# Four chained vision layers on one core: each tile's gathers are sent once those of the tile before have landed

## The reference

```python
x = x + moe(gn(x))           # layer 0: 2x2 patches, 8 experts, top 2
x = x + relu(bn(deform(gn(x))))   # layer 1
x = x + ssm_glu(gn(x))       # layer 2: 16-tap state-space convolution, GLU
x = x + convnext(gn(x))      # layer 3: 7x7 depthwise convolution, MLP

def deform(x):
    dy, dx, mask = conv3x3(x, w_om) + b_om         # 9 offsets and 9 masks a pixel
    py, px = base_y + dy, base_x + dx
    # bilinear: four corners of each of the 9 places, at data-dependent indices
    sampled = sum(gather(x, corner) * weight(corner) for corner in four) * sigmoid(mask)
    return einsum('bckhw,ock->bohw', sampled, w) + b
```

## Time and profile before

| | |
|---|---|
| timed runs, median of 3 (lowest to highest) | 1748.08 us (1746.49 to 1748.33) |
| span of the profiled execution | 2176.8 us |
| the profiled execution's own time | no other than its span is given |
| first and last start of a gather, profiled | 78.2 us, 1983.5 us |
| mean granted TensorE clock, profiled | 0.801 of full speed |
| POOL busy, profiled | 1190.0 us, of it gathers 1135.1 us |
| PE, DVE, ACT busy, profiled | 1392.0, 953.2, 526.5 us |

### The profile page before, as it was taken

The page is one execution under the profiler, slowest core; times in us unless marked ns, Lnnn a source line. Parts: engine busy times, 40 slices in busy tenths (PEclk is TensorE's granted clock), DMA queues, the critical chain, the costliest instruction groups (busy, mean ns, idle before and its releaser), DMA issues.

```text
span 2176.8 us, 13143 instructions
## 1 busy us (share of the span) xinstructions
PE 1392.0 (64%) x3780; PEld 595.6 (27%) x3780; DVE 953.2 (44%) x1562; ACT 526.5 (24%) x860; POOL 1190.0 (55%) x1393
## 2 busy tenths in 40 slices
PE   4647554496246877863366878855368874386976
PEld 3433212242112333322122333322123321132322
DVE  2424233354341333884532323875323328532564
ACT  1111111121112233211222333211213322132544
POOL 8655446357665555676565454676645566673000
PEclk9868766698567998986577889977678987687987
DMA  5212212132241111222141111222221112110100
GB/s 192 60 48 68 52 40 62 49 90 59 74 101 41 43 44 43 71 66 58 53 113 46 31 40 39 74 65 58 57 76 35 41 44 57 41 58 26 32 5 18
DMA packets 111591, 123.70 MB, mean 57 GB/s; under 512 B 50720, under 2 KB 88224, under 8 KB 111136
## 3 DMA queue, kind: packets, MB, share of 16 engines
q0 software_dynamic: 36864, 75.57, 12.5%
q1 hardware_dynamic: 73600, 43.82, 8.1%
q10 hardware_dynamic: 1056, 3.47, 0.4%
HBM read 99.79 MB, written 9.01 MB: 50 GB/s over the span
## 4 chain that ended last, share of the span: by engine, by line
PE 36%; another core or an unknown queue 27%; DVE 16%; issue 12%; ACT 7%; DMA 1%; SPq 1%; ACTq 0%; DVEq 0%
PE bank L1795 7%; PE bank L1808 7%; PE bank L1721 4%; DVE rb L1599 3%; PE bank L1717 3%; PE bank L1731 3%; DVE gt L1508 3%; PE bank L1752 2%; PE bank L1831 2%; PE bank L1783 2%; PE bank L1817 1%; DVE he L1406 1%; PE bank L1847 1%; PE bank L1772 1%
## 5 line engine op out<-in xcount | busy, mean ns | idle before, releaser
L1055 POOL DMA_INDIRECT gt<-corner_table,idx x1152 | 1135.1, 985 | 783.8 <-DVE sm L1516 392.4
L1795 PE MATMUL bank<-u,wk 128*128 128x512 f32 x512 | 256.7, 648 | 25.6 <-issue 9.6
L1808 PE MATMUL bank<-yg,wts 128*128 128x512 f32 x512 | 241.6, 615 | 46.9 <-ACT yg L1189 30.2
L1406 DVE SCALAR_TENSOR_TENSOR he<-he,bank 128x512 f32<-128x512 f32 (+1 forms) x144 | 90.2, 627 | 275.4 <-remote 88.9
L1721 PE MATMUL bank<-xg,w_sb 128*128 128x512 f32 (+1 forms) x288 | 149.3, 602 | 85.0 <-DVE xg L1397 61.9
L1772 PE MATMUL bank<-cst,sm 128*128 128x128 f32 x384 | 80.0, 322 | 187.0 <-ACT st L1173 79.7
L1540 DVE SCALAR_TENSOR_TENSOR tg<-tg,ae 128x512 f32<-128x512 f32 x64 | 44.5, 696 | 344.3 <-ACT ae L1201 270.9
L1731 PE MATMUL bank<-he,w_sb 128*128 128x512 f32 (+1 forms) x288 | 143.0, 580 | 54.6 <-DVE he L1406 30.9
L1508 DVE TENSOR_TENSOR gt<-gt,bank 128x1152 f32<-128x1152 f32 x128 | 172.5, 1347 | 0.9
L1599 DVE SCALAR_TENSOR_TENSOR rb<-xp,par,rb 128x1024 f32<-128x1024 f32 x124 | 155.1, 1291 | 0.0
L1125 ACT ACTIVATE he<-bank 128x512 f32<-128x512 f32 (+1 forms) x144 | 78.8, 549 | 294.3 <-PE bank L1717 166.7
(11 more groups left out here) (222 smaller groups left out, 1390.2 us busy)
## 6 DMA issues: line engine op xcount, KB each, us to landing
gt<-corner_table,idx POOLq DMA_INDIRECT x1152
tb<-gate_of_token SPq DMA_DIRECT2D x32, 256.0 KB
sqb<-gate_of_token SPq DMA_DIRECT2D x24, 256.0 KB
u<-sqb SPq DMA_DIRECT2D x48, 128.0 KB
corner_table<-tb SPq DMA_DIRECT2D x36, 128.0 KB, 2.7
w_sb<-w ACTq DMA_DIRECT2D x2, 1024.0 KB, 6.7
sqb<-gate_of_token SPq DMA_DIRECT2D x16, 128.0 KB
u<-xg SPq DMA_DIRECT2D x16, 128.0 KB
```

What stands on the lines that cost most here:

```text
L1055: pool.indirect_dma_start(gt[:, t % GRING, k].rearrange("p a c -> p (a c)"), None, corners, bass.IndirectOffsetOnAxis(ap=idx[s % 2][:, j, ...
L1406: stt(out=he[:, u % 2, 0:w], in0=he[:, u % 2, 0:w], scalar=1.0, in1=psum[b][:, 0:w], op0=ALU.add, op1=ALU.mult).then_inc(free[b], 1)
L1795: op = mm(psum[b][:, :], wk[:, t, d], u4[:, g, at:at + HALF], start=t == 0, stop=t == JJ - 1 and n > 0)
L1808: op = mm(psum[B2.bank(*name)][:, :], w_glu[:, k, col + d * P:col + (d + 1) * P], yg[:, c % 2, k], start=k == 0, stop=k == NB2 - 1)
```

## The change

Before the nine gathers of a tile, POOL also waits until all nine of the preceding tile have landed. `u` is the running number of the preceding tile, and its semaphore has by then been raised nine times by 16 in each of its `u // GRING + 1` turns. The first tile of step 0 has none before it.

```diff
                 if s or t >= GRING:
 
                     pool.wait_ge(S["smp_ready"], FROM + s * NT * GI + t - GRING + 1)
+                if s or t:
+                    u = s * NT * GI + t - 1
+                    pool.wait_ge(gathered[u % GRING], (u // GRING + 1) * 16 * KK)
                 for k in range(KK):
                     pool.indirect_dma_start(
```

## The result

The changed kernel takes **2044.3 us** (2042.62 to 2048.8, 4 runs) beside 1748.2 us for the kernel before in the same session: 1.1702 times, 95% interval 1.1683 to 1.1722. It is 296 us slower. The forecast was slower, at 1896 us with a range up to 1930. Half of the loss was foreseen.

The account below looks back on a forecast made before the run. POOL, sending gathers nearly without a pause, was taken as the bound; 1748.1 us + 146 for 120 paying waits + 10 for late landings - 8 absorbed = 1896 us, range 1765 to 1930 us (its own range 1860 to 1930).

Parts of the forecast that it names:

- What bounds the kernel: In timed runs POOL sends gathers nearly without a pause, one each 1.25 us; its summed time is 1738 us.
- Rival (1): The wait is hidden because the timed POOL is not the bound: 1748 to 1751 us; chance 0.13.
- The wait itself costs nothing: The added wait instruction on POOL, one among waits already there before a tile's first gather, was put at nothing.
- What one wait costs: At a tile boundary on POOL, 1.52 us instead of the 0.30 us gap: 1.22 us a tile.
- Late landings: Gathers queued behind SP's `u4` loads may land up to 10 us late; 10 us taken, bounds 0 and 60.
- How many pay: Of 127 added waits, 7 run under POOL's waits for table or indices; 120 pay, 146 us.
- Absorbed by POOL's idle time: The idle time POOL still has in timed runs, 10 us, absorbs 8 us of the cost.
- Rival (3): The landing is told late, as for SP's table store: 1.73 us a tile, 208 us, 1956 us; chance 0.04.
- What is late next: Nothing new: each tile reaches DVE 1.2 us later, and the 192 us after the last tile move as a whole.
- the ring: POOL's ring of four buffers doesn't help, since it lets POOL run ahead only if POOL is the faster one.
- Rival (2): POOL bounds some stretches, PE or DVE the others: 1821 us with half the boundaries, 1765 to 1855; chance 0.17.
- What the profile would show: Gaps between tiles at least about 1.4 us, inside tiles 0.30; profiled span up by perhaps 0 to 60 us.

Follow-up runs that it names:

- second profile: The kernel before, unchanged, run and profiled once more: 1751.0 us, 1.0011 times, with a profiled span of 1749.2 us.
- the run with eight gathers: Ninth gather left out from the fifth tile on, against the kernel before: 1718.8 us, 0.9832 times; with the change's wait as well, 1888.7 us, 1.0817 times.

## Why the prediction was right in sign and short in size

**What bounds the kernel: right.** The argument took the first profile's span for an execution unlike the timed ones, dropped POOL's 392.4 us for `smp_ready`, and found 1738 us. The second profile shows POOL as the argument had it, with 8.4 us of such waits and a tail of 168.8 us instead of 192.4. That the sum came within 10 us is partly luck. The second profile has 1,143 gaps of 0.30 us, 348.5 us, where the sum took 330, and 0.3 us of waiting for the table where it kept 19.7; these two cancel. The other misses are 8 us each for longer gathers and for `smp_ready`, 7 us the other way for the tail, and 1.5 us ahead of the first gather.

Rival (1) is out by the 296 us. Its evidence, 10.2 us of slack of DVE before tile 59, was not room on POOL. The second profile, in which POOL has none, still shows much of it: the last gather of tile 59 ends at 784.9 us, and DVE takes the tile at 792.6 us.

```profile
783.91 0.95 POOL L1055 DMA_INDIRECT gt<-corner_table,idx  x1 [0.30 <-issue]
...
792.58 1.34 DVE L1508 TENSOR_TENSOR gt<-gt,bank 128x1152 f32<-128x1152 f32 x1
```

That is some 6 us after the landing. DVE has to wait at 16 other tiles of that profile, and at none of the first: slack in one stretch does not tell of the others. The rule of the Trainium skill that was cited with this reading ("Perfetto Trace Analysis", GPSIMD Engine Instruction: go by start-to-start spacing, not by length) is borne out. By the lengths, 0.94 us, POOL had a quarter of room; by the 1.25 us spacing it had none, and the runs agree with the spacing.

**The wait itself costs nothing: right.** Waiting two tiles back cost 0.0%.

**What one wait costs: the step that failed.** The prediction had 1.25 us to the landing, 0.27 us to the restart, less 0.30: 1.22 us a tile. The change's 127 pauses are 2.58 us on average, less 0.30: 2.28 us. Term by term:

- Last packet after the gather's end: 1.25 us taken, 1.23 measured (median). Right.
- From the last packet to the semaphore's full count: nothing taken, 0.32 us measured. The small packets were taken for the count itself, and their end for its arrival. 0.32 x 127 = 41 us.
- From the count to POOL's start: 0.27 us taken, from a wait for DVE that the gather carried itself. Measured 0.74, and 0.26 when the waits are exchanged. 0.47 x 127 = 60 us. The change leaves the gather carrying `smp_ready` and puts the open wait in an instruction of its own. The prediction took its row from the other kind, and the diff does not show the difference.
- Late landings: 10 us taken, 37 us measured (the pauses above 2.6 us, by what they exceed the median of 2.29). Only the `u4` loads had been thought of, and gate shares were the more frequent. 37 - 10 = 27 us.
- How many pay: 120 taken, 127 measured, 9 us. The waits for table and indices at the starts of steps, which were to hide seven, are not in the second profile: 0.3 us for the table, and the one for indices is ahead of the first tile, which has no added wait.
- Absorbed by POOL's idle time: 8 us taken. Right: the 8.4 us for `smp_ready` are gone in the changed kernel.

41 + 60 + 27 + 9 = 137 us. The other 13 us are gathers that took longer (1156.7 us busy beside 1143.5); 234 of them took over 1 us, 183 in the kernel before. The forecast's growth was 148 us; 148 + 137 + 13 = 298, and 296 was measured.

Part of the miss was in a row at hand. Rival (3), by the row of SP's table stores, priced a landing told late at 1.73 us a tile and 208 us in all, and got a chance of 0.04. The landing is told 2.5 us (median) after the start of the gather, and 2.7 was that row's figure. It was nearer to the truth than the packets were, and should have had more weight. It would not have been enough: its 1956 us is still 88 us below what was measured, since it had neither the slower restart nor the late landings beside gate shares. The Trainium skill ("DMA: Bandwidth & Descriptors", Anatomy of one DMA: about 2.0 us plus the bytes over 436 GB/s, mostly the confirmation of the last write) gives 2.15 us for 64 KB. Counted from the gather's start that is 0.35 us too little. Counted from its end, as the prediction's sentence also tried, it made 2.12 us a tile, near to the measured 2.28, but for another reason: the runs show 1.55 us to the landing and 0.74 to the restart.

**What is late next, and the ring: right.** A wait at every second tile costs half, and the tail is unchanged. **Rival (2)** (hidden in part) is out for this kernel, and the run with eight gathers shows where it becomes true: with 133 us of room, 126 of the 296 are hidden.

**What the profile would show:** the gaps inside a tile stayed at 0.30 us and those between tiles are above 1.4, as said. That the changed kernel's profiled span would grow far less than the timed median rested on its having the first profile's lateness again. It did not have it, and its span fell below the first one's.

**Open.** Why the first profiled execution was late is not known; the second, of the same program, was not. That trace also holds only a third of the DMAs' semaphore updates that the second one has (7,630 beside 23,951). Why a restart from a separate wait takes 0.48 us longer was not taken further than its dependence on the order of the waits. Why the gathers themselves took 13 us longer was not tried; two profiles of the kernel before differ by 8 us in this (1135.1 and 1143.5), so part of it may be no effect of the change.

## What to carry to other kernels

Where an engine sends without a pause, a wait for its own transfer costs what is left from the last issue until it runs again, and that has four parts: packets, the count's arrival, the restart, and the late ones among the landings. Take the first three from a row in which that engine waits for that kind of transfer, by the same kind of wait, and not from packets. Where there is none, the nearest row with a whole landing in it tells of the first two, and the restart and the late landings come on top. Setting the wait two sends later brought the cost from 296 us to 13.

When a profile is a quarter longer than the timed runs, take it again before reasoning on its slack. In the two traces of one program POOL's idle time before gathers differed by 412 us: the first showed room for this change, and the second none.

## What the runs showed of the hardware

- An indirect DMA of 64 KB issued by POOL shows its first packet 0.71 us after the instruction's end, its last 1.23, and its semaphore's full count 1.55 us (medians over the 127 boundaries of the changed kernel; the count from the 123 where it was recorded whole). In the other runs that wait for a landing the count came 1.51 to 1.53 us after the end.
- POOL started a gather 0.26 us after the awaited count when the gather carried the wait, and 0.74 us after it when the open wait was an instruction of its own and the gather carried another, already met. Exchanging the two waits in the source brought the one to the other and 43 us. DVE, waiting for the same counts, started 0.02 us after them (median of 89), 0.09 in the boundary shown.
- A wait that is met when it is reached cost nothing that could be measured: 1.0002 times with 126 of them.
- A pause of POOL behind SP's transfers: 3.4 to 4.9 us beside a gate share of 256 KB, 8.2 and 7.8 us beside shares and `u4` loads together, 3.8 us beside `u4` loads alone, where the median is 2.29.
